# Turning the context's keys with VectorE and moving them by DMA, in a perceiver block on one core

## The reference

```
x = x + xattn(layernorm(x), ctx)                  # ctx: [64, 257, 512]
  q = layernorm(x) in 16 heads of 32; k = v = ctx in 16 heads of 32
  sim = q @ k.T / sqrt(32); out = softmax(sim) @ v; out @ W_out.T + b_out
x = x + self_attention(layernorm(x))              # low-rank q and kv, rotated columns
x = x + expert[argmax(layernorm(x) @ Wg)](...)    # 8 experts, 512 -> 512 -> 512, gelu
```

## Time and profile before

| what | us |
|---|---|
| median of 2 runs | 949.0 (948.46 to 949.54) |
| the profiled execution's own time | 948.3 |
| its span, first to last instruction | 946.1 |
| outside the span | 2.2 |
| first `exp` on ACT starts at | 13.39 |
| stores of the first and of the 13th tile are issued at | 156.43 and 648.29 |

### The profile page before, as it was taken

One profiled execution on the slowest core, in us unless ns is written; L12 is line 12 of the kernel. 1 busy time (PEld: TensorE's weight loads), 2 busy tenths in 40 slices (PEclk: granted clock), 3 DMA queues, 4 the chain that ended last, 5 costly groups with the idle time before them and its releaser, 6 DMA issues.

```text
span 946.1 us, 27317 instructions
## 1 busy us (share of the span) xinstructions
PE 853.3 (90%) x11224; PEld 644.3 (68%) x11224; DVE 523.7 (55%) x1127; ACT 436.3 (46%) x1083; POOL 314.5 (33%) x661
## 2 busy tenths in 40 slices
PE   5997989999999999999999999999976459999998
PEld 3554767767686776868777686777765347777775
DVE  2565456565656656566665656656543343554552
ACT  2444455555645555464555646455532123343332
POOL 2022323233332323232332423233231045666553
PEclk9998999999999999999999999999987569999999
DMA  9512121112212112122212212211050189433330
GB/s 316 185 47 58 46 78 60 58 60 78 69 58 80 57 58 84 55 69 70 68 58 66 82 54 65 77 58 58 2 189 12 42 280 387 130 94 99 111 93 3
DMA packets 40074, 85.40 MB, mean 90 GB/s; under 512 B 9230, under 2 KB 10510, under 8 KB 39952
## 3 DMA queue, kind: packets, MB, share of 16 engines
q1 hardware_dynamic: 34048, 71.58, 23.1%
q0 software_dynamic: 3680, 10.23, 3.2%
q10 hardware_dynamic: 2224, 1.86, 0.7%
HBM read 75.27 MB, written 10.22 MB: 90 GB/s over the span
## 4 chain that ended last, share of the span: by engine, by line
PE 72%; DVE 9%; ACT 8%; issue 6%; POOL 3%; ACTq 1%; DMA 0%; DVEq 0%; POOLq 0%
PE bank L414 9%; PE scores L1351 9%; PE bank L1366 8%; PE bank L416 7%; PE bank L415 7%; PE scores L459 6%; PE bank L472 4%; PE bank L447 4%; PE bank L408 3%; PE bank L485 3%; ACT soft_block L764 3%; ACT prob L717 2%; DVE negmax L919 2%; POOL operand_lo L1156 2%; PE bank L623 2%
## 5 line engine op out<-in xcount | busy, mean ns | idle before, releaser
L717 ACT ACTIVATE prob<-scores,negmax 128x257 f32<-128x257 f32 x256 | 119.3, 472 | 161.9 <-DVE negmax L919 160.9
L919 DVE TENSOR_REDUCE negmax<-scores 128x2 f32<-128x514 f32 x128 | 88.2, 689 | 151.4 <-PE scores L459 151.4
L414 PE MATMUL bank<-qkv_hi,operand_hi 128*128 128x396 f32 x256 | 103.0, 402 | 0.0
L1351 PEld LDWEIGHTS scores<-rows_t,w 128*128 128x128 f32 x736 | 87.7, 196 | 11.6 <-issue 10.5
L415 PE MATMUL bank<-qkv_lo,operand_hi 128*128 128x396 f32 x256 | 88.9, 347 | 0.0
L416 PE MATMUL bank<-qkv_hi,operand_lo 128*128 128x396 f32 x256 | 88.8, 347 | 0.0
L459 PE MATMUL scores<-k_t,q_t 32*32 32x257 f32 x2048 | 86.9, 395 | 1.9 <-ACT prob L717 0.5
L1351 PE MATMUL scores<-rows_t,w 128*128 128x128 f32 x736 | 87.9, 279 | 0.7 <-ACT rows_t L1389 0.7
L447 PE MATMUL bank<-consts,context 128*128 128x128 f32 x512 | 79.7, 279 | 4.5 <-ACT k_t L702 4.4
L1366 PE MATMUL bank<-w_all,hidden 128*128 x184 | 82.8, 592 | 0.0
L472 PE MATMUL bank<-consts,prob 128*128 128x128 f32 x512 | 81.1, 281 | 0.0
(11 more groups left out here) (211 smaller groups left out, 1744.0 us busy)
## 6 DMA issues: line engine op xcount, KB each, us to landing
context<-in_ctx SPq DMA_DIRECT2D x64, 512.0 KB, 3.8
w_all<-in_L_ffn_W SPq DMA_DIRECT2D x16, 1024.0 KB, 8.3
b<-in_L_ffn_b SPq DMA_DIRECT2D x23, 256.0 KB
x_tile<-in_x SPq DMA_DIRECT2D x16, 256.0 KB, 3.8
x_scratch<-x_tile SPq DMA_DIRECT2D x16, 256.0 KB, 2.0
soft_block<-in_L_xattn_W_out SPq DMA_DIRECT2D x1, 1024.0 KB, 12.1
late<-in_L_attn_Wk_r_w SPq DMA_DIRECT2D x1, 1024.0 KB, 14.4
soft_block<-in_L_attn_Wo_w SPq DMA_DIRECT2D x1, 1024.0 KB, 5.1
```

What stands on the lines that cost most here:

```text
L414: pe.matmul(to, op_hi[op][:, c, :], w_hi[name][:, c, columns], start=(c == 0), stop=False)
L717: act.activation(prob[pair][:, gg, :], scores[:, gg, 0:J], ACT.Exp, bias=negmax[b % 2][:, g:g + 1], accum_out=sums[t % 2][:, g, bl:bl + 1] ...
L919: dve.tensor_reduce(negmax[b % 2][:, 2 * pair:2 * pair + 2], scores[:, :, 0:J], AX.X, ALU.max, negate=True).then_inc(maxed, 1)
L1351: done = pe.matmul(scores[:, m // 2, (m % 2) * P:(m % 2 + 1) * P], w1[h * G + k][:, m * P:(m + 1) * P], rows_t[h][:, k, :], start=(k == 0) ...
```

## The change

It does five things.

1. TensorE no longer turns the context. VectorE turns it in blocks of 32x32: `turn_keys(b, c)`, one instruction of 128x512 for each half c of the keys, into `k_blocks`. A block then still lies on the partitions of its keys' quarter r, not on those of its head hl.
2. 16 DMAs from SBUF to SBUF, one for each (r, hl), of 32 partitions by 1 KB, bring the blocks to the heads' partitions in `k_t[b % 2]`. SP issues them (`bring_keys`, step 7, two batches ahead); for batches 0 to 3 ACT does. There is one `k_blocks`: `turn_keys(b)` waits until batch b-1 has been brought, and `bring_keys(b)` until b is turned and batch b-1 has been scored. In the loop it is batch b+2 that is turned and brought while batch b is scored and attended.
3. The last key is scored by itself, from `last_t`: 8 more products with one column for each pair, ahead of the 8 with 256 columns. `move_last` goes.
4. `context_bank` becomes a fourth bank of the stages; the queries are turned into one of them, at the new offset QUERIES, and `bank_of` and the offsets of the stages are set anew.
5. `x_tile` 2 and 3 are one tensor that the unit preparation uses for `down[0]`; so their loads wait for the unit "rot".

The core of the diff, in the order constants, tensors, SP (`bring_keys`), TensorE (`score`), ACT (the two loops that issue DMAs: the first ahead of its steps, the second for batches 2 and 3), VectorE:

```
+SELF, ..., RANK, QUERIES) = (
+    -6, -1, -6, -1, 1, 4, 3, 4, 6, 0, 10, 14, 14, 18, 23, 20, 33, 37, 42, 43, 42, 48, 44, 50, 54, 60, 83, 87, 88, 94, 112, 114, 118, -48)
-TURN_C_AT = (2, 7)
-TURN_P_AT = (5, 10)
+KEYS_AT = (0, 4)
+BRING_AT = 7
+TURN_P_AT = (4, 10)
-KEEP_AT = (4, 10)
+KEEP_AT = (8, 10)
...
-    k_t = [sbx(f"k_t{i}", [P, 2, J]) for i in range(2)]
+    k_t = [sbx(f"k_t{i}", [P, 4, C2, G, HD]) for i in range(2)]
+    k_blocks = sbx("k_blocks", [P, HL, C2, G, HD])
...
-    prob_bank, context_bank, att_bank, banks = psum[0], psum[1], psum[2], psum[3:6]
+    prob_bank, att_bank, banks = psum[0], psum[1], psum[2:6]
...
+    def piece_of(b, n):
+        r, hl = divmod(n, HL)
+        return k_t[b % 2][hl * HD:(hl + 1) * HD, r, :, :, :], k_blocks[r * HD:(r + 1) * HD, hl, :, :, :]
...
+        def bring_keys(b):
+            until.wait_ge(keys_turned, 2 * b + 2)
+            until.wait_ge(scored, 2 * (b - 1))
+            for n in range(4 * HL):
+                sp.dma_start(*piece_of(b, n)).then_inc(keys_brought[b % 2], 16)
...
         def score(b, pair):
-            until.wait_ge(k_moved[pair], b + 1)
+            until.wait_ge(keys_brought[b % 2], BRINGS * (b // 2 + 1))
...
+                    pe.matmul(scores[place * S:(place + 1) * S, gg, J - 1:J], q_t[rows, g, bl, :], last_t[rows, g, b:b + 1], start=True, stop=True)
...
+                    done = pe.matmul(scores[place * S:(place + 1) * S, gg, 0:J - 1], q_t[rows, g, bl, :],
+                                     k_t[b % 2][rows, :, :, g, :].rearrange("p r c k -> p c r k"), start=True, stop=True)
...
+        for b in range(2):
+            until.wait_ge(keys_turned, 2 * b + 2)
+            for n in range(4 * HL):
+                act.dma_start(*piece_of(b, n)).then_inc(keys_brought[b % 2], 16)
...
+            if k == BRING_AT and b + 2 < BT:
+                until.wait_ge(keys_turned, 2 * (b + 2) + 2)
+                until.wait_ge(scored, 2 * (b + 1))
+                for n in range(4 * HL):
+                    act.dma_start(*piece_of(b + 2, n)).then_inc(keys_brought[b % 2], 16)
...
+        def turn_keys(b, c):
+            until.wait_ge(context_loaded[b % 4], 16 * (b // 4 + 1))
+            until.wait_ge(keys_brought[(b - 1) % 2], BRINGS * ((b - 1) // 2 + 1))
+            dve.transpose(k_blocks[:, :, c, :, :], context[b % 4][:, c, :].rearrange("p (g h d) -> p h g d", g=G, h=HL)).then_inc(keys_turned, 1)
...
             if k == SCORE_AT[0] and b < B:
                 largest(b, 0)
+            for c in range(C2):
+                if k == KEYS_AT[c] and b + 2 < B:
+                    turn_keys(b + 2, c)
             if k == SCORE_AT[1] and b < B:
                 largest(b, 1)
```

More of the change, by code:

```diff
@@ L193, in program @@
     w_lo = {n: sba(f"{n}_lo", [P, G, w], F32R) for n, w in widths}
-    x_tile = [sba(f"x_tile{i}", [P, D]) for i in range(4)]
+    x_pair = sba("x_pair", [P, 2, D])
+    x_tile = [sba(f"x_tile{i}", [P, D]) for i in range(2)] + [x_pair[:, i, :] for i in range(2)]
     norm_x, norm_w, norm3 = (sba(n, [P, D]) for n in ("norm_x", "norm_w", "norm3"))
@@ L232, in program @@
     rot_q, rot_k = sba("rot_q", [P, 2, 2, ROPE]), sba("rot_k", [P, G, 2, ROPE])
-    down = [sbx("down0", [P, 2, D]), late[:, 4:6, :]]
+    down = [x_pair, late[:, 4:6, :]]
     staged_c, staged_d = sbx("staged_c", [P, G, D]), late[:, 0:4, :]
@@ L378, in sync_program @@
                 load_context(b + 3)
+            if k == BRING_AT and BT <= b + 2 < B:
+                bring_keys(b + 2)
             if step == UNIT_AT[4]:
@@ L425, in bank_for, with turn_queries @@
             return banks[bank_of[stage]]
-        def place_queries(t):
-            until.wait_ge(const_loaded, 16)
-            until.wait_ge(normed_x, t + 1)
[L430 to L448, removed]
+        def turn_queries(t):
+            if t:
+                bank = bank_for("queries", t)
+            else:
+                until.wait_ge(const_loaded, 16)
+                bank = banks[bank_of["queries"]]
+            until.wait_ge(normed_x, t + 1)
+            turn(norm_x, bank, queries_turned)
         def score(b, pair):
@@ L532, in stages @@
         def stages(step):
+            t = tile_at(step, QUERIES)
+            if t >= 1:
+                turn_queries(t)
             t = tile_at(step, SPREAD)
@@ L720, in stages @@
         def stages(step):
+            t = tile_at(step, QUERIES)
+            if t >= 1:
+                place_queries(t)
             t = tile_at(step, ATT_HI)
@@ L812, in scalar_program @@
                 load_small()
-            if k == TURN_C_AT[0] and b + 1 < B and 0 not in DVE_KEYS:
-                move_keys(b + 1, 0)
             if k == SCORE_AT[1] and b < B:
@@ L1061, in vector_program @@
         measure(x_tile[0][:, :], "x", measured_x)
-        move_keys(0, 1)
+        for b in range(2):
+            for c in range(C2):
+                turn_keys(b, c)
         for step in range(LAST_STEP):
@@ L1067, in vector_program @@
                 largest(b, 0)
-            if k == TURN_C_AT[0] and b + 1 < B and 0 in DVE_KEYS:
-                move_keys(b + 1, 0)
+            for c in range(C2):
+                if k == KEYS_AT[c] and b + 2 < B:
+                    turn_keys(b + 2, c)
             if k == SCORE_AT[1] and b < B:
@@ L1333, in turn_rows @@
         def turn_rows(s):
-            bank = (prob_bank, context_bank)[s % 2]
+            bank = (prob_bank, att_bank)[s % 2]
             until.wait_ge(normed_e, s + 1)
```

84 lines of the change are left out of this document (25 added, 59 removed).

## The result

The changed kernel takes 1248.24 us (median of 2 runs, 1246.12 to 1250.37) against 949.0: a ratio of 1.3153, interval 1.3052 to 1.3255. It is slower by almost a third. The profiled execution took 1250.37 us with a span of 1248.2.

A forecast was written before the change was run, and what follows sets the result against it. TensorE's own work was taken to bound the steady part, with the keys' loop just above it after the change. 948.3 - 11 (14 tiles at -0.8) + 16 (start) = 953.3, given as 953 us; range 918 to 1000.

The forecast's parts named there:

- the keys' loop: Turning and bringing keys through one k_blocks cannot overlap itself: 39.7 us a tile, 0.2 above TensorE's bound; 40.2 taken.
- rival B: SP's 16 issues between two batches' turns become the bound: 990 or 1034 us, deciding from 0.43 us an issue; chance 0.25.
- The issue: SP's time to start one piece in the keys' loop: 0.41 us, between 0.37 and 0.54.
- The landing: From the last piece's issue start to its arrival, in the keys' loop: 1.25 us, between 1.2 and 2.0.
- The start: First exp waits behind both first bringings in ACT's program: at 28.2 us, 14.8 later; start together +16 us (+10 to +24).
- rival C: The start costs little because later work catches up: +4 instead of +16 us, 941 us; chance 0.08.
- ACT's bursts for batches 2 and 3: ACT's issuing of these batches' pieces at step 7, during preparation: 6.7 us each, 1.5 us each counted as cost.
- TensorE's work: Per tile, turns leaving give -3.5 us, one-column products add 2.0: bound 41.0 to 39.5, or 38.0 if waits end.
- rival D: One-column products on TensorE cost as much as a scoring group (0.59 us): bound 42.2 us a tile, 981 us; chance 0.07.
- Rival A: Issues in the keys' loop cheap or hidden, TensorE last at 38.0 us a tile: 916 us; chance 0.18 including up to 930.
- The clock: TensorE's granted clock between the 1st and 13th store: read as 1.00, the higher level, 2.4 GHz.
- signs named ahead: New profile: L447 gone from TensorE, SP bursts of 16 lasting 6 to 7 us, first turn waiting, stores 40.2 us apart.

The follow-up runs named there:

- Experiment 4: The kernel before, with SP bursts of four kinds (SBUF or DRAM source, fewer bytes, more rows) into a spare tensor nobody waits for: 944.36 us, ratio 1.0005.
- experiment 2: The changed kernel with 8 of each batch's 16 pieces issued by ACT instead of SP from batch 4 on: 1171.05 us.
- numbers 3 and 5 to 7: 3: changed kernel's blocks via DRAM in 5 issues, 965.23 us; 5: that with old table, 978.86; 6: 5 plus first keys by TensorE, 967.54; 7: 3 plus those, 951.72.
- experiment 9: The changed kernel with only 8 of the 16 pieces brought from batch 4 on, the other half of the keys left as it was: 983.81 us.
- experiment 8: The kernel before with one part alone: the last key scored by itself with one-column products and move_last gone: 953.65 us, ratio 1.0086.
- experiments 10 to 12: 10, 11: number 7 with VectorE's turns and the issues at other steps, 963.22 and 962.98 us; 12: number 7, second turn cut to one block from batch 8, 948.48.

## Why the prediction was wrong

The forecast was 953 us with a range to 1000, and 1248 came. The mechanism stood in the text twice, as the keys' loop and as rival B. Its formula, 4 x (turns + bringing) + 3.7, is right: with the measured 15 x 0.69 + 1.9 + 0.2 = 12.5 for bringing it gives 4 x (1.4 + 12.5) + 3.7 = 59.2 us a tile, and 59.4 were measured. (That it meets within 0.2 is partly luck: the stages between the turns take a little less than 3.7, and in some batches the last landing takes over 3 us.) The failure is one of sizes, and of a range whose ends came from the wrong rows.

- **The issue** (taken 0.41, bounds 0.37 to 0.54; measured 0.69). This is the step that failed: 15 x 0.28 = 4.2 us a batch, 17 us a tile, over 14 tiles some 235 of the 295 us by which I missed. I had argued that a piece has 32 rows where a store has 128, and that the DMA engines are idle. Experiment 4 shows that the rows don't set the price, and that an issue is as dear in bursts on SP's queue that nobody waits for. Of the 0.28 us some 0.22 are the median (0.59 and the gap), the other 0.06 the few issues of over 1 us. The issue of the earlier trace rows and the load of the earlier trace rows have DRAM at one end and stand alone or behind one other, while every burst in the trace was dearer; the earlier trace rows hold 0.69 us for six loads in a row. I quoted it and explained it away by tiny pieces. That it is the very number is chance as far as the runs show, as those loads read DRAM. The trace of before had no SBUF to SBUF transfer at all, so the upper bound had to be that row, and with it the loop would have come to 4 x (1.4 + 10.35 + 1.25 + 0.2) + 3.7 = 56.5 us a tile: the range would have reached to a time near 1185, 948.3 + 14 x 15.5 + 20, still 63 short of the measured one.
- **The landing** (taken 1.25, bounds to 2.0; measured 1.9): another 0.65 x 4 = 2.6 us a tile, 36 in all. I had subtracted the transfer from the stores' 2.0 us; a piece with an eighth of the bytes lands only 0.1 us sooner. The Trainium skill, "DMA: Bandwidth & Descriptors", section "Anatomy of one DMA", has some 2.0 us as a part that does not depend on the bytes, for another issuing path; the 1.8 to 1.9 here, into SBUF and from SP's queue, agree with it better than my split did.
- **Rival B** was said to decide from 0.43 us an issue, and it did; but it was priced at 990 and 1034, with 0.41 and 0.46, and most of its weight was on the milder form. The Trainium skill, "DMA: Bandwidth & Descriptors", section "Issuing engines are not separate DMA queues", says that an engine's time to start a DMA is usually small beside the DMA. Here 16 issues are 11.08 us against 1.9 for the last to land, so it does not hold for a set of small pieces. The same section says that issuing on several engines saves the issuing time only; experiment 2 agrees, with 54.9 us a tile in place of 59.4.
- **The start** (first exp at 28.2; measured 36.15). The terms, from ACT's queue and VectorE:

```profile
9.10 10.23 ACTq L812 DMA_DIRECT2D k_t<-k_blocks  x16
...
25.95 10.15 ACTq L812 DMA_DIRECT2D k_t<-k_blocks  x16
...
36.15 0.48 ACT L719 ACTIVATE prob<-scores,negmax 128x257 f32<-128x257 f32 x1 [26.68 <-issue]
```
```profile
24.62 1.30 DVE L912 STREAM_TRANSPOSE k_blocks<-context 128x512 f32<-128x512 f32 x2 [15.89 <-DMA k_t<-k_blocks]
```

  Two bursts of 10.2 in place of 7.7 give 5.0 of the 8 us, the landing in the rush of the start (5.9 instead of 3.0) the rest. The order of events was as forecast. That the late start is paid almost in full, against rival C, is what the medians of numbers 3 and 5 to 7 say.
- **ACT's bursts for batches 2 and 3** were put at 6.7 us each and 1.5 on the path. The one for batch 2 lasts 12.2 us (42.07 to 54.24). The first store is 77 us late: 23 by the first exp, 41 by SP's bursts from batch 4 on (experiment 9), so some 13 are left for ACT's two bursts and what else the start has. The loop holds from the first tiles on and not, as I had it, from the third.
- **TensorE's work** was right in sign and its terms too dear by a little. The one-column products were taken at 0.25 us for each pair; experiment 8 shows 0.05. In the changed kernel 13 of the 16 begin within 0.09 us ahead of the first product with 256 columns, the others between the next ones:

```profile
568.58 0.24 PE L465 MATMUL scores<-last_t,q_t 32*32 32x1 f32 x13
568.67 0.38 PE L470 MATMUL scores<-k_t,q_t 32*32 32x256 f32 x1
...
569.24 0.44 PE L432 MATMUL bank<-qkv_hi,operand_hi 128*128 128x396 f32 x1
```

  The whole group takes 0.66 us from start to start against 0.59. That excludes rival D's price (0.59 more). But the second half of my step, that a tile follows TensorE's bound down, did not hold even without the loop: in numbers 3 and 7 the tile stays at 40.9 us. What took back the gain of the turns stays open (experiments 10 to 12). Rival A would have failed on this, too.
- **The clock.** I took the higher level for granted. In the changed kernel the granted clock is 0.82 between the 1st and the 13th store, where the earlier trace rows have 1.00. Behind an idle stretch of 4.22 us TensorE's dense products have a granted clock of 0.50 (window 562 to 563), the lower level of 1.2 GHz, with 0.33 us from start to start, and some 6 us later 1.00 (568.0 to 569.3), with 0.18:

```profile
561.70 0.70 PE L432 MATMUL bank<-qkv_hi,operand_hi 128*128 128x396 f32 x1 [4.22 <-DVE logits L1038]
562.20 0.53 PE L433 MATMUL bank<-qkv_lo,operand_hi 128*128 128x396 f32 x1
562.53 0.53 PE L434 MATMUL bank<-qkv_hi,operand_lo 128*128 128x396 f32 x1
...
568.13 0.34 PE L433 MATMUL bank<-qkv_lo,operand_hi 128*128 128x396 f32 x1
568.31 0.34 PE L434 MATMUL bank<-qkv_hi,operand_lo 128*128 128x396 f32 x1
```

  It makes TensorE's busy time larger (43.0 us a tile in place of 38.9). It costs nothing that shows here: between the two stores the chain that ended last goes to 66% through SP's issues and to 15% through landings, and has no line of TensorE.

Of the signs named ahead, the turns gone from TensorE, the bursts of 16, the waiting first turn and the unhindered second one are there. Bursts of over 7 us and later landings, which the text had named as ways to be wrong, came, and the stores stand 59.4 us apart, not 40.2.

Two slips in the prediction have no bearing on this: the DMA engines are at work in slices 17 to 29 of the earlier trace rows, not to 30, and the range starts at 918 as "A's end", where A's sum gives 916.

## What to carry to other kernels

Count the DMAs that one engine has to start inside a loop that cannot overlap itself, and price each at what a *burst* in the trace costs, from the same kind of memory to the same kind; a single issue in an idle queue is no such row, and when there is none, take the dearest burst as the bound. When data have to change partitions, a trip through DRAM with few large DMAs (5 issues, 965 us) can beat many direct pieces (16 issues, 1248 us). And work taken off the engine that is last can give nothing back: here TensorE lost 2.4 us of work a tile (38.9 to 36.5) and the tile stayed as long, with more of VectorE's stages in the chain that ended last. What would win it back was not found.

## What the runs showed of the hardware

- An issue on SP's queue from SBUF to SBUF takes 0.51 us (0.56 in the first kind of experiment 4) at the head of a burst and 0.59 behind another, on ACT's 0.51 and 0.61; with DRAM as the source it is 0.33 and 0.42 for the same 32 rows of 1 KB. These are medians. 32 or 128 partitions, 256 bytes or 1 KB a row make no difference (experiment 4), nor does a second queue that issues at the same time (experiment 2).
- Some issues take over 1 us, up to 2.1, on both queues: about one in 14 of the changed kernel's on SP's queue, one in 9 of experiment 4's reads from DRAM. They lift the mean from 0.59 to 0.65. The cause stays open.
- The burst is also paid by what comes behind it: a store or a load right after one takes 0.58 us, the store at 233.54 among them, where it takes 0.33 alone.
- A 32 KB piece from SBUF to SBUF lands 1.8 to 1.9 us after its issue starts in a quiet phase.
- A one-column product on 32x32 weights costs next to nothing: 0.05 us on the path for 8 of them (16 instructions).
